# Second normalisation, its transposes and the router product put into the following slot of a software pipeline; output chain spread over more steps; small statistics operations on GpSimd

## The reference

```python
x = x + jnp.tanh(g_xattn[0]) * _L0_xattn_ref(_layernorm(x), ctx_1024, ctx_1024, Wq, bq, Wk, bk, Wv, bv, Wo, bo)
x = x + jnp.tanh(g_ffn[0]) * _L0_ffn_ref(_layernorm(x), Wg, W1, W2)      # experts choose tokens
x = x + jnp.tanh(g_xattn[1]) * _L1_xattn_ref(_layernorm(x), ctx_1024, Wq, Wkv)   # no output product
x = x + jnp.tanh(g_ffn[1]) * _L1_ffn_ref(_layernorm(x), gate_w, w1, b1, w2, b2)  # top 2 of 8

scores = jnp.einsum('bhqd,bhkd->bhqk', Q, K) * scale
out = jnp.einsum('bhqk,bhkd->bhqd', jax.nn.softmax(scores), V)           # first layer: then out @ Wo.T + bo
logits = xt @ Wg                                                         # router, on the second normalisation
```

## Time and profile before

| | us |
|---|---|
| median of three runs | 875.13 |
| the profiled execution | 874.29 |
| its span, first to last instruction | 872.5 |
| TensorE busy | 536.8 (62%) |
| VectorE busy | 484.0 (55%) |
| ScalarE busy | 349.5 (40%) |
| GpSimd busy | 285.4 (33%) |

### The profile page before, as it was taken

One profiled execution on the slowest core, in us unless ns is written; L12 is line 12 of the kernel. 1 busy time (PEld: TensorE's weight loads), 2 busy tenths in 40 slices (PEclk: granted clock), 3 DMA queues, 4 the chain that ended last, 5 costly groups with the idle time before them and its releaser, 6 DMA issues.

```text
span 872.5 us, 16776 instructions
## 1 busy us (share of the span) xinstructions
PE 536.8 (62%) x5459; PEld 427.9 (49%) x5459; DVE 484.0 (55%) x1521; ACT 349.5 (40%) x795; POOL 285.4 (33%) x342
## 2 busy tenths in 40 slices
PE   1688999987200008862798999861000199999960
PEld 0566666664100007651566667640000199999960
DVE  4668888874588203434789999847200034444324
ACT  1157777766100004321266777762000055555530
POOL 6102222201001754771011111010777435555550
PEclk9979999999555559995699999995555599999995
DMA  7543333320000312325455553200311212222219
GB/s 251 151 136 88 87 88 88 88 58 2 0 0 3 101 55 81 106 77 137 124 144 148 158 153 97 59 2 2 101 53 52 62 53 73 75 71 75 74 37 288
DMA packets 94628, 76.37 MB, mean 88 GB/s; under 512 B 13904, under 2 KB 88528, under 8 KB 94096
## 3 DMA queue, kind: packets, MB, share of 16 engines
q1 hardware_dynamic: 86432, 57.05, 24.0%
q0 software_dynamic: 7040, 14.53, 4.9%
q10 hardware_dynamic: 1072, 3.73, 1.3%
HBM read 45.54 MB, written 33.46 MB: 91 GB/s over the span
## 4 chain that ended last, share of the span: by engine, by line
PE 41%; POOL 15%; DVE 12%; issue 10%; DMA 9%; ACT 7%; SPq 4%; ACTq 1%; DVEq 0%; POOLq 0%
POOL dispatched L407 10%; PE bank L730 8%; PE bank L740 8%; PE bank L683 6%; PE bank L577 4%; PE bank L551 4%; POOL returned L414 4%; PE bank L565 4%; DMA QS_N<-MH 3%; DVE PT L979 2%; DVE MX L789 2%; ACT N L496 2%; DMA returned<-PT,META_ROW 2%; ACT PT L443 2%; PE bank L630 1%
## 5 line engine op out<-in xcount | busy, mean ns | idle before, releaser
L789 DVE TENSOR_REDUCE MX<-bank 128x4 f32<-128x512 f32 x256 | 172.9, 685 | 45.0 <-PE bank L577 44.8
L443 ACT ACTIVATE PT<-bank 128x512 f32<-128x512 f32 x256 | 152.7, 600 | 107.2 <-PE bank L565 106.4
L414 POOL DMA_INDIRECT returned<-PT,META_ROW x124 | 119.1, 961 | 111.8 <-DVE PT L1070 87.1
L521 ACT ACTIVATE XGT<-bank 128x256 f32<-128x256 f32 x62 | 23.8, 384 | 260.3 <-PE bank L551 260.3
L551 PE MATMUL bank<-CONST,PT 128*128 128x128 f32 x124 | 25.9, 292 | 148.2 <-issue 142.1
L577 PE MATMUL bank<-KS,QS_N 96*128 96x128 f16 x1024 | 104.8, 229 | 12.1 <-DMA KS<-spread 10.0
L565 PE MATMUL bank<-QS_N,KS 98*128 98x512 f16 x256 | 99.2, 391 | 8.2 <-DMA QS_N<-MH 7.8
L740 PEld LDWEIGHTS bank<-WALL,HT 128*128 128x128 f32 x808 | 98.8, 192 | 10.2 <-issue 7.0
L740 PE MATMUL bank<-WALL,HT 128*128 x808 | 101.1, 276 | 3.9 <-issue 1.5
L730 PE MATMUL bank<-XGT,XT_HL_WR 128*128 128x256 f32 x404 | 100.7, 389 | 0.0
L577 PEld LDWEIGHTS bank<-KS,QS_N 96*128 96x128 f16 x1024 | 78.5, 104 | 34.1 <-DMA KS<-spread 11.6
(11 more groups left out here) (172 smaller groups left out, 830.5 us busy)
## 6 DMA issues: line engine op xcount, KB each, us to landing
spread<-XT_HL_WR SPq DMA_DIRECT2D x128, 64.0 KB, 2.1
PT<-dispatched SPq DMA_DIRECT2D x62, 130.0 KB, 2.1
QS_N<-spread SPq DMA_DIRECT2D x128, 48.0 KB
KS<-spread SPq DMA_DIRECT2D x32, 192.0 KB
WALL<-in_w SPq DMA_DIRECT2D x8, 578.0 KB, 4.0
CT<-in_ctx SPq DMA_DIRECT2D x32, 128.0 KB, 2.7
spread<-XT_HL_WR SPq DMA_DIRECT2D x32, 128.0 KB, 2.3
dispatched<-in_pads SPq DMA_DIRECT2D x2, 1040.0 KB, 5.7
```

Source lines behind the costliest of these rows:

```text
L414: pool.indirect_dma_start(ys[layer][:, :], bass.IndirectOffsetOnAxis(ap=META_ROW[:, a.f, c:c + 1], axis=0), YS[:, a.f, c, :], None).then_i ...
L443: nc.scalar.activation(PT[:, c, 4 * g:4 * g + 4, :].rearrange("p j q -> p (j q)"), ST[i % 2][:, :], ACT.Exp, scale=SCALE[layer]).then_inc( ...
L789: V.tensor_reduce(out=MX[:, m.u, 2 * J * g + c:2 * J * (g + 1):2], in_=MB[i % 2][:, :].rearrange("p (j k) -> p j k", j=J), op=ALU.max, axi ...
```

## The change

The four engine functions of the attention slot are rewritten in order and partly in age:

- N (the second normalisation), its transposes and n_copied go from `z` in step 6 and 7 to `y` in step 0 and 2 of the next slot; the NT copy, the router product and LG follow in steps 3, 4 and 5 of that slot instead of steps 0, 2 and 3. LG's product now goes to PF, not PA.
- RC and OK go from `b` at the end of a slot to `z` in step 1 of the next. The transposes of OK go from step 0 to 2, OKT from 1 to 2 (behind exponential 6), the output product from 2 to 4, the update of x from 3 to 5, STATS_N from 4 to 7.
- XN's transposes go from step 1 to 0, XT's copy keeps its place behind exponential 5 (before: 6), the values products from steps 0 and 4 to 1 and 5, the value product L647 from 5 to 6, OT's transposes from 6 to 7. The transpose of MX goes ahead of `scores(b, 4)`.
- On VectorE statistics of `n` go from step 1 to 2, XN from 6 to 4, HL from 5 to 6.
- VE, MINUS and VE_N (two columns each) go from VectorE to GpSimd, and there the second normalisation comes last in the slot.

```diff
@@ gpsimd
                     if n:
                         ...
+                        chain.link(nc.gpsimd.tensor_scalar(out=VE[:, n.u, :], in0=MV[:, n.u, :, 1], scalar1=LN_EPS, scalar2=None, op0=ALU.add))
                         nc.gpsimd.tensor_tensor(out=RSTD[:, n.u, :], in0=VE[:, n.u, :], in1=EXPO[:, :], op=ALU.pow).then_inc(x_rstd, 1)
                     ...
+                    if z:
+                        pool.wait_ge(n_stats, z.g + 1)
+                        pool.wait_ge(n_copied, before(z.g - 1))
+                        nc.gpsimd.tensor_scalar(out=MINUS[:, z.u, :], in0=MV_N[:, z.u, :, 0], scalar1=-1.0, scalar2=None, op0=ALU.mult)
+                        chain.link(nc.gpsimd.tensor_scalar(out=VE_N[:, z.u, :], in0=MV_N[:, z.u, :, 1], scalar1=LN_EPS, scalar2=None, op0=ALU.add))
+                        chain.link(nc.gpsimd.tensor_tensor(out=RSTD_N[:, z.u, :], in0=VE_N[:, z.u, :], in1=EXPO[:, :], op=ALU.pow))
...
@@ scalar
                     exponentials(b, 4)
                     if y:
-                        act.wait_ge(n_t, y.g + 1)
-                        act.wait_ge(lg_done, y.g)
-                        nc.scalar.activation(NT[:, :], PF[:, 256:512], ACT.Copy).then_inc(n_kept, 1)
+                        act.wait_ge(n_rstd, y.g + 1)
+                        for c in range(2):
+                            last = nc.scalar.activation(N[:, y.b + c, 0:D], batch(y, c), ACT.Identity,
+                                                        scale=RSTD_N[:, y.u, c:c + 1], bias=OFFSET_N[:, y.u, c:c + 1])
+                        last.then_inc(n_copied, 1)
...
@@ tensor
                     scores_for_maxima(2)
                     scores(b, 6)
                     ...
+                    if y:
+                        pe.wait_ge(n_copied, y.g + 1)
                         if m:
                             pe.wait_ge(v_kept, m.g + 1)
+                        if f:
+                            pe.wait_ge(front_kept, f.g + 1)
+                        pe.wait_ge(lg_kept, y.g)
                         for c in range(2):
+                            last = transpose(PF[:, 256 + c * P:256 + (c + 1) * P], N[:, y.b + c, 0:D])
+                        last.then_inc(n_t, 1)
...
@@ vector
                     maxima(7)
-                    if b:
-                        dve.wait_ge(o_t, b.g + 1)
...
+                    if z:
+                        dve.wait_ge(x_new, z.g + 1)
+                        dve.wait_ge(n_stats, z.g)
+                        dve.wait_ge(n_copied, before(z.g - 1))
+                        stats(z, STATS_N, MV_N[:, z.u]).then_inc(n_stats, 1)
```

More of the change, by code:

```diff
@@ L587, in slot @@
                         transpose(PG[0:32, 256:256 + P], MX[:, a.u, :]).then_inc(m_t, 1)
+                    scores(b, 4)
+                    if f:
+                        pe.wait_ge(x_norm, f.g + 1)
+                        if m:
+                            pe.wait_ge(v_kept, m.g + 1)
+                        for c in range(2):
+                            last = transpose(PF[:, c * P:(c + 1) * P], XN[:, f.u, c * D:(c + 1) * D])
+                        last.then_inc(front_t, 1)
+                    scores_for_maxima(1)
+                    scores(b, 5)
                     if b:
                         values(b, 0)
+                    scores_for_maxima(2)
+                    scores(b, 6)
                     if z and layer == 0:
@@ L635, in slot @@
                     scores(a, 0)
-                    if b:
+                    if z and layer == 0:
+                        pe.wait_ge(ok_kept, z.g + 1)
+                        for c in range(2):
+                            last = nc.tensor.matmul(PO[:, 256 + c * P:256 + (c + 1) * P], OKT[:, c * P:(c + 1) * P],
+                                                    WSQ[:, 3, :], start=True, stop=True)
+                        last.then_inc(wo_done, 1)
+                    if y:
+                        pe.wait_ge(n_kept, y.g + 1)
+                        for c in range(2):
+                            last = nc.tensor.matmul(PF[:, 256 + E * c:256 + E * c + E], NT[:, c * P:(c + 1) * P],
+                                                    WG[:, layer, :], start=True, stop=True)
+                        last.then_inc(lg_done, 1)
+                    scores_for_maxima(5)
+                    scores(a, 1)
+                    if b:
+                        values(b, 1)
+                    scores_for_maxima(6)
+                    scores(a, 2)
+                    if r:
+                        pe.wait_ge(front_kept, f.g + 1 if f else r.g + 1)
                         if y:
                             pe.wait_ge(lg_kept, y.g + 1)
-                        values(b, 1)
-                    scores_for_maxima(5)
-                    scores(a, 1)
-                    if r:
-                        pe.wait_ge(front_kept, f.g + 1 if f else r.g + 1)
                         pe.wait_ge(v_kept, r.g)
@@ L801, in slot @@
                     maxima(1)
+                    if z:
+                        dve.wait_ge(o_t, z.g + 1)
+                        dve.wait_ge(x_new, z.g)
+                        if layer == 0:
+                            dve.wait_ge(ok_t, z.g)
+                        o = PO[:, :].rearrange("p (h w) -> p h w", w=2 * HD)
+                        link(V.reciprocal(RC[:, :], o[:, :, HD]))
+                        V.tensor_tensor(out=OK[:, :].rearrange("p (h d) -> p h d", d=HD), in0=o[:, :, 0:HD],
+                                        in1=RC[:, :].unsqueeze(2).broadcast_to([P, 2 * H, HD]), op=ALU.mult).then_inc(o_kept, 1)
+                    maxima(2)
                     if n:
@@ L804, in slot @@
                         dve.wait_ge(x_stats, n.g)
-                        link(stats(n, STATS, MV[:, n.u]))
-                        V.tensor_scalar(out=VE[:, n.u, :], in0=MV[:, n.u, :, 1], scalar1=LN_EPS, scalar2=None,
-                                        op0=ALU.add).then_inc(x_stats, 1)
-                    maxima(2)
+                        stats(n, STATS, MV[:, n.u]).then_inc(x_stats, 1)
                     maxima(3)
+                    maxima(4)
+                    if n:
+                        dve.wait_ge(x_rstd, n.g + 1)
+                        dve.wait_ge(front_t, before(n.g - 1))
+                        for c in range(2):
+                            last = V.tensor_scalar(out=XN[:, n.u, c * D:(c + 1) * D], in0=batch(n, c), scalar1=MV[:, n.u, c, 0:1],
+                                                   scalar2=RSTD[:, n.u, c:c + 1], op0=ALU.subtract, op1=ALU.mult)
+                        last.then_inc(x_norm, 1)
+                    maxima(5)
                     if z:
@@ L819, in slot @@
                                                    in1=two(z).rearrange("p c d -> p (c d)"), op0=ALU.mult, op1=ALU.add).then_inc(x_new, 1)
-                    maxima(4)
-                    if z:
-                        dve.wait_ge(x_new, z.g + 1)
-                        dve.wait_ge(n_stats, z.g)
-                        dve.wait_ge(n_copied, before(z.g - 1))
-                        link(stats(z, STATS_N, MV_N[:, z.u]))
-                        V.tensor_scalar(out=MINUS[:, z.u, :], in0=MV_N[:, z.u, :, 0], scalar1=-1.0, scalar2=None, op0=ALU.mult)
-                        V.tensor_scalar(out=VE_N[:, z.u, :], in0=MV_N[:, z.u, :, 1], scalar1=LN_EPS, scalar2=None,
-                                        op0=ALU.add).then_inc(n_stats, 1)
-                    maxima(5)
+                    maxima(6)
                     if f:
```

84 lines of the change are left out of this document (15 added, 69 removed).

## The result

On the chip where the two were timed beside each other the changed kernel takes 883.1 us (median of 4 runs, 881.2 to 884.8) against 875.1 before (874.2 to 876.3): ratio 1.0090, 95% interval 1.0064 to 1.0115. It is slower, by 0.9%; 869.6 was predicted, with a range of 862 to 878. The profiled execution took 884.76 us round its span of 882.9.

A forecast was written before the change was run, and what follows sets the result against it. TensorE and VectorE, both nearly full, bound the kernel before; after the change a ring would set full slots. First stage -5.1 and second -0.4 make -5.5 us: 869.6 us against the median, range 862 to 878.

The forecast's parts named there:

- The ring: Block 6, HL, statistics, GpSimd, N and XT copies, N transposes, back to block 6: sets slots at 10.80 and 10.07 us.
- The first rival: Full slots: the round across engines doesn't bind, slots take 10.5 and 9.1 us, 857 us in all; chance 0.12.
- GpSimd's MINUS and VE_N ... I take 0.38: Hand-over of the second normalisation's statistics on GpSimd: 0.38 us, taken between 0.31 and 0.48.
- the upper end: GpSimd's MINUS and VE_N strictly behind each other, 0.20 each with the 0.08 of a link: 0.48 us.
- XT to TensorE 0.43: Full slots: from ScalarE's XT copy to TensorE's transposes of N, 0.43 us.
- The second rival: GpSimd's small operations cost more: 892 us at 0.7 each, mild form 872 to 880; chance of the whole 0.16.
- The lower end: GpSimd's MINUS and VE_N overlapping like independent memsets: 0.03 + 0.20 + 0.08 = 0.31 us.
- the ends: Slots 13 to 15 and the chain to the last LG: 3.8 us gained in first stage, 0.7 in second.
- 0.1 for GpSimd's two operations: First stage's end: 8.6 us of dependent steps, today's plus 0.1 for two operations on GpSimd instead of VectorE.
- In the second, by the same steps (... N in the way), 0.7: Second stage's end: gains 0.7 us, without OK transposes and product to move apart, N in the way.
- The first two are held by the DMA of MH, which doesn't move: First stage, slots 0 to 2: 0.9 us less, the first two slots still held by MH's transfer.
- The third rival: Nothing comes of the stage ends, only full slots count: 877 us, with half of it 873 to 876; chance 0.20.

The follow-up runs named there:

- experiment 1: Changed kernel with VE, MINUS and VE_N back on VectorE: 879.6 us, ratio 1.0036 to the kernel before.
- experiment 2: Changed kernel with ScalarE's XT copy ahead of exponential 5 and the N copies: 867.9 us, ratio 0.9923 to the kernel before.
- the second kernel of experiment 9: Changed kernel with XT's copy first, small operations on GpSimd in layer 0 and VectorE in layer 1, pads behind their slot's other transfers: 890.8 us, ratio 0.9880.
- experiment 7: The changed kernel once more, unedited, on the chip where the kernel before takes 901.4 us: 910.6 us in one run.
- experiment 4: Changed kernel with layer 0's two 1 MB pad transfers issued at pairs 13 and 14 instead of 0 and 1: 880.4 us, ratio 1.0043.
- experiment 5: Changed kernel with the pad transfers in slots 0 and 1 but behind the slot's other transfers, on another chip: 907.4 us, ratio 1.0072.
- experiment 3: Kernel before with only VE, MINUS and VE_N moved to GpSimd: 878.7 us, ratio 1.0029.
- experiment 10: Changed kernel, XT's copy first, MINUS and VE_N on VectorE, OK before MH in layer 0: 888.6 us; with MX's transpose later as well: 892.1 us.

## Why the prediction was wrong

- **The ring: right in kind.** Place and releaser of the waits in the full slots, and the absence of one at OT, came as forecast; experiments 1 and 2 shorten it by what their pieces say, and the slots are the same on another chip. The first rival (the ring doesn't bind) is out.
- **The ring's length: wrong, and this is the first step that failed.** "GpSimd's MINUS and VE_N ... I take 0.38" measured 0.59, above the 0.48 that stood as the upper end. "XT to TensorE 0.43" measured 0.62. These are 0.21 and 0.19 us a slot; with 0.12 less for TensorE's steps and 0.04 more for the rest the walk is 0.32 longer than forecast. Over ten slots it is 0.35 a slot in the first stage and 0.42 in the second, 7.7 us over twenty. The second rival had said that the gain would be gone from 0.28 more per slot.
- **Where the two prices came from.** The lower end for the pair rests on memsets that start 0.03 apart, another kind of instruction: these two start 0.29 apart. The upper end leaves out the 0.08 behind the second operation, which the lower end counts; with it, it is 0.56 and nearly right. The 0.43 is what a copy of this size took before, from OKT's start to its product at 141.25, 0.05 behind the copy's end:

```profile
140.82 0.38 ACT L456 ACTIVATE OKT<-bank 128x256 f32<-128x256 f32 x1
```

  N's transposes start 0.25 or more behind XT's end (144.72 to 144.97 here) in all twenty full slots. Why it is not 0.05, no run shows.
- **The Trainium skill,** "GPSIMD Engine Reference", section Performance versus the Vector engine, spoke against tiny operations there, and the trace agrees: 0.59 us for the pair there, 0.32 on VectorE. I had let the rule weigh no more than 0.10 us a slot; moving the operations cost 0.28 to 0.36 (experiment 1). The same page's sentence that one instruction's completion does not hold back the next (section Instruction dispatch) says nothing of how soon the next starts, and I had read the memsets' 0.03 into it.
- **The ends: the second step that failed.** With the slots as measured and all else as forecast the sum is 877.3, still within 862 to 878; the ends (-3.8 and -0.7 forecast, -0.9 and +3.4 in the profiles) and the head take it out. In the first stage slots 13 to 15 came as forecast (17.7; 18.0). The end, 22.4 forecast, took 25.8 with the granted clock at 0.78, 23.6 at 0.91 in the second kernel of experiment 9, and 22.3 at 0.89 in experiment 1, where the small operations are on VectorE. So both the clock, which the forecast took as before, and the "0.1 for GpSimd's two operations" seem to be in the miss; the runs don't part them. In the second stage the length of work was wrong too: without any dip in slots 13 to 15 they and the end take 40.1 us (experiment 7), 37.6 forecast. "In the second, by the same steps (... N in the way), 0.7" put too little on N: the wait for it behind the last MH is 1.30 us.
- **The head of the first stage: wrong.** "The first two are held by the DMA of MH, which doesn't move": TensorE's two waits for it grew by 1.42 and 1.30 us, and from pair 0's MH to pair 3's became 1.0 longer instead of 0.9 shorter. That TensorE waits there because of the pads is shown (experiments 4 and 5). Why it waits longer than before is open: at the first wait the pad goes out 0.67 us ahead of MH's transfer instead of 1.33, but at the second the distance is 0.64 in both kernels.
- **The third rival** (ends give nothing, 877) was right about the ends of this profile and had the slots too short.
- **A slip without effect:** TensorE's own work stands as 9.35 us in one place and 9.44 in the sums. With the ring out of the way (experiment 2) the slots less their waits are 9.53, and 8.9 in the second stage, where 8.6 was taken.

What stays open: what decides in a given run whether the clock falls at the ends (waits of nearly the same length went with it and without it), and what the second stage's longer end is made of beyond the wait at N. Whether the longer waits for MH in experiment 3 come from the edit is open too.

## What to carry to other kernels

When a change closes a ring (a round of instructions on several engines that must pass before the next slot's can), its length decides, and pieces that no row shows should be taken at the dear end: the pieces summed to 10.80 and measured 11.12, and those 3% alone turn the sign (877.3 against 875.1). Count the hand-over behind the last piece too. A pipeline's ends need their own walk, and another one for a lower clock. Before moving small work to a free engine, look for the queue in the ring that does something else first; here one swap in ScalarE's queue turned +0.9% into -0.8%. And once one ring is shortened, the next limit (OK, then the transfer of MH) stands close behind.

## What the runs showed of the hardware

- A 128x2 TENSOR_SCALAR on GpSimd is busy 0.22 to 0.23 us and the next independent one starts 0.29 later; on VectorE 0.16 to 0.17, and 0.08 later.
- A chip on which the kernel before takes 901 us instead of 875 gave the attention slots of the changed kernel the same to 0.02%; the difference lies in routing and experts (214.6 against 198.1 us between the stages, 292.1 against 280.7 behind the second).
- Adding matmuls held the clock (0.95 instead of 0.78 over the first stage's end) and shortened that end by 0.7 us only (25.1 against 25.8).
- An 8 KB transfer of MH landed 1.8 us after its issue in the median of the first stage's full slots, and up to 3.7 us in those of experiment 10.
